# Value products of an attention unit in two steps instead of four, in a two-layer transformer kernel on one core

## The chip, the core and the metric

The kernel runs on one NeuronCore of a Trainium2 chip. The core has a matrix engine (TensorE, PE in the profile; its weight loads are the separate row kind PEld), and three engines for elementwise work: VectorE (DVE), ScalarE (ACT) and GpSimd (POOL). SyncE (SP) issues DMAs. Each engine works through its own list of instructions in order, and the engines hand over by semaphores. The metric is device time in microseconds from one launch; the time before is the median of three runs, 6809.92 us (6809.24 to 6820.73).

## The reference

Sixteen batches of 1024 tokens with 128 channels pass through a token embedding, attention layer zero (8 heads of 64, with a group norm ahead of it), a triangular MLP, attention layer one (8 heads of 16) and a top-1 mixture of 16 experts. What matters here is the attention of either layer:

```
scores = einsum('bhqe,bhke->bhqk', Q, K) * scale
attn   = softmax(scores, axis=-1)
out    = einsum('bhqk,bhke->bhqe', attn, V)
```

The kernel takes the softmax with a row maximum that is computed first, and divides by the sum at the end: the sum is an extra column of ones in V.

## The kernel before

**Units and steps.** A unit is one head and one half of its queries (512): 16 units for each batch and layer. A unit has eight steps, `kt` 0 to 7, one for each 128 keys. In each step PE makes one 128x512 tile of raw scores for a later unit's row maximum (`max_tile`, L884), then the scores of this step's keys: in layer zero two matmuls (L910 and L912), in layer one a single one (L912). DVE reduces the maximum tile (L1630), ACT takes the exponential of the scores (L1143) and writes them to `pr`. For layer zero POOL makes the low part of the exponentials (`lo_parts`, L506), four pieces a unit.

**Value products.** The products with V belong to the unit before (`at - 1`), so they run beside the scores of the present unit. `VALUE_STEPS` says in which four steps; part `j` of 0 to 3 goes to `VALUE_STEPS[j]`. For a layer-zero unit (`values0`) each part is 16 matmuls (8 pairs of L929 and L930, 128x129 in bf16) for 128 queries. For a layer-one unit (`values1`) parts 0 and 1 are four column-packed fp32 matmuls each (L945), that add up in the same bank, and part 3 is `fold1` (L955): ACT first copies the bank to `oT` (L1160), and four more matmuls then turn and sum the four quarters. Part 2 is empty there. ACT's copy stands in ACT's list at step 4 behind the exponential of that step (`OUT_STEPS = (4, 7)`).

**The banks.** Scores, maximum tiles, value outputs and the rest ("glue": projections, transposes, MLP and expert matmuls) have two PSUM banks each. So tile k of the maxima waits until tile k-2 is reduced (`max_reduced`), and the scores of step k wait until the exponential of step k-2 is done (`exp_done`).

**Segments.** The program is five segments: `first` (layer zero of batch 0), `second`, `loop` (13 turns), `penult` (each with both layers, 32 units) and `final` (layer one of the last batch). In those of two layers the units go: four of layer zero, then layer one and layer zero in turn (12 pairs), then four of layer one. Other work ("beside") is issued behind the values of a step by tables of steps: among it, in the loop, a pair of expert matmuls (L870) at steps 0 and 1 of most units, whose results DVE adds at steps 2 and 3 (L1620).

**Order inside a step on PE:** the maximum tile, the scores, the values if the step has any, the row turn (L890), the work beside.

Of the kernel before, what the change touches and what calls it, by code (L numbers as in the profile page):

```python
# [28 lines left out]
def units_of(kind):  # L29

    if kind == "first":
        return [(0, u) for u in range(16)]
    if kind == "final":
        return [(1, u) for u in range(16)]
    pairs = [unit for i in range(16 - LEAD) for unit in ((1, i), (0, LEAD + i))]
    return [(0, u) for u in range(LEAD)] + pairs + [(1, u) for u in range(16 - LEAD, 16)]
# [45 lines left out]
def due_tiles(kind, step):  # L82
    return DUE_TILES[kind].get(step, [])


def due_rows(kind, step):
    return DUE_ROWS[kind].get(step, [])
# [238 lines left out]
def build(nc, x, tok_w, gn_w, gn_b, wq, bq, wk, bk, wv, bv, wo, bo, w1, b1, w2, b2,  # L326
# [14 lines left out]
    with ExitStack() as ctx:  # L341
# [137 lines left out]
        def await_drained(eng, seg, *names):  # L479
            plan = PLANS[seg.kind][0]  # L480
            for b in range(2):
                uses = [plan[name][1] for name in names if plan[name][0] == b]
                if uses:
                    eng.wait_ge(glue_drained[b].sem, glue_drained[b].at(seg, max(uses) + 1))
# [23 lines left out]
        def steps_of(kind):  # L508
            for at, (layer, u) in enumerate(units_of(kind)):
                for kt in range(T):  # L510
                    yield 8 * at + kt, at, layer, u, kt
# [162 lines left out]
        def _(te):  # L674
# [198 lines left out]
            def max_tile(seg, when, layer, head, n):  # L873
                b = seg.layer(layer) if when == "now" else seg.following(layer)
                k = TILE_PLACES[seg.kind][when, layer, head, n]
                t, g = n // 2, n % 2
                if n == 0:
                    await_stack(te, b, layer, head)
                te.wait_ge(max_reduced.sem, max_reduced.at(seg, k - 1))
                if layer == 0:  # L880
                    qs, ks = qA[:, head % 2], kA[:, head % 2]
                else:
                    qs, ks = q_stack(1, head), k_stack(1, head)
                mm(maxb[k % 2][:, :], qs[:, t * P:(t + 1) * P], ks[:, g * HALF:(g + 1) * HALF],  # L884
                   start=True, stop=True).then_inc(max_filled.sem, 1)
# [6 lines left out]
            def tiles_and_rows(seg, step):  # L892
                for tile in due_tiles(seg.kind, step):
                    max_tile(seg, *tile)
                for it in due_rows(seg.kind, step):
                    turn_row(seg, *it)

            def turn_row(seg, when, layer, head, g):
                b = seg.layer(layer) if when == "now" else seg.following(layer)
                max_turn(seg, row_name(when, layer, head, g), b, layer, head, g)  # L900

            def scores(seg, at, layer, u, kt):
                b, k, head, g = seg.layer(layer), 8 * at + kt, u // 2, u % 2
                if kt == 0:
                    arrived = mrow_in[2 * layer + g]
                    te.wait_ge(arrived.sem, arrived.at(b, 16 * (head + 1)))
                te.wait_ge(exp_done.sem, exp_done.at(seg, k - 1))
                bank, q, kk = score[k % 2], slice(g * HALF, (g + 1) * HALF), slice(kt * P, (kt + 1) * P)
                if layer == 0:
                    mm(bank[:, :], kA[:, head % 2, kk], qA[:, head % 2, q], start=True, stop=False)  # L910
                last = max_row(0) + 1 if layer == 0 else P
                mm(bank[:, :], k_stack(layer, head)[0:last, kk], q_stack(layer, head)[0:last, q],  # L912
                   start=(layer == 1), stop=True).then_inc(score_filled.sem, 1)

            def values0(seg, at, j):
                _, u = units_of(seg.kind)[at]
                head, w = u // 2, 2 * D0 + 1
                n = o_place(seg.kind, 0, u, j // 2)
                if j == 0 and u % 4 == 0 and u > 0:
                    await_drained(te, seg, f"v0c{u // 4}.0", f"v0c{u // 4}.1")  # L920
                if j == 0:
                    te.wait_ge(lo_done.sem, lo_done.at(seg.l0, 4 * (u + 1)))
                if j % 2 == 0:
                    te.wait_ge(o_drained.sem, o_drained.at(seg, n - 1))
                dst = obank[n % 2][:, (j % 2) * 256:(j % 2) * 256 + w]
                for kt in range(T):
                    hi = pr[:, at % 2, kt, j * P:(j + 1) * P].bitcast(BF16).rearrange("p (q two) -> p q two", two=2)[:, :, 1]
                    lo = low_of(u, kt - kt % 2)[:, kt % 2, j * P:(j + 1) * P]
                    mm(dst, hi, v0[:, head // 2 % 2, kt, head % 2, 0:w], start=(kt == 0), stop=False)  # L929
                    last = mm(dst, lo, v0[:, head // 2 % 2, kt, head % 2, 0:w], start=False, stop=(kt == T - 1))  # L930
                if j % 2 == 1:
                    last.then_inc(o_filled.sem, 1)

            def values1(seg, at, j):
                _, u = units_of(seg.kind)[at]
                n = o_place(seg.kind, 1, u)
                te.wait_ge(exp_done.sem, exp_done.at(seg, 8 * at + 4 * j + 4))
                if j == 0 and u == 0:
                    await_drained(te, seg, "v1.0", "v1.1")
                if j == 0:  # L940
                    te.wait_ge(o_drained.sem, o_drained.at(seg, n - 1))
                col = (D1 + 1) * (u // 2)
                for r in range(4):
                    kt = 4 * j + r
                    last = mm(obank[n % 2][QUAD * r:QUAD * (r + 1), :], v1[:, kt, col:col + QUAD], pr[:, at % 2, kt, :],  # L945
                              start=(j == 0), stop=(j == 1))
                if j == 1:
                    last.then_inc(o_filled.sem, 1)

            def fold1(seg, at):  # L950
                _, u = units_of(seg.kind)[at]
                n = o_place(seg.kind, 1, u)
                te.wait_ge(o_hi_out.sem, o_hi_out.at(seg, n + 1))
                for t in range(4):
                    last = mm(obank[n % 2][:, QUAD * t:QUAD * (t + 1)], oT[:, t * P:(t + 1) * P], fold[:, :],  # L955
                              start=True, stop=True)
                last.then_inc(oT_turned.sem, 1)

            def values(seg, at, j):
                if units_of(seg.kind)[at][0] == 0:  # L960
                    values0(seg, at, j)
                elif j < 2:
                    values1(seg, at, j)
                elif j == 3:
                    fold1(seg, at)

            def attention(seg, *beside):
                for step, at, layer, u, kt in steps_of(seg.kind):
                    for tile in due_tiles(seg.kind, step):
                        max_tile(seg, *tile)  # L970
                    scores(seg, at, layer, u, kt)
                    if at > 0 and kt in VALUE_STEPS:
                        values(seg, at - 1, VALUE_STEPS.index(kt))
                    for it in due_rows(seg.kind, step):
                        turn_row(seg, *it)
                    for work in beside:
                        work.run(step)
                for j in range(4):
                    values(seg, at, j)
                for step in range(step + 1, LAST[seg.kind]):  # L980
                    tiles_and_rows(seg, step)
                    for work in beside:
                        work.run(step)
                if seg.nxt:
                    await_drained(te, seg, "v0c0.0", "v0c0.1")
# [735 lines left out]

LAST_STEP = 1000
LO_STEPS = (2, 4, 6)
VALUE_STEPS = (2, 3, 5, 6)
OUT_STEPS = (4, 7)
STORE_STEPS = {"loop": 191, "penult": 191, "final": 124}
SCALES = (64 ** -0.5, 1.0 / math.sqrt(16))
# [46 lines left out]
```

## Time and profile before

| what | value |
|---|---|
| median of three runs | 6809.92 us |
| profiled execution, its own time | 6804.59 us |
| its span (first to last instruction) | 6802.8 us |
| mean granted TensorE clock | 0.951 |
| PE busy | 6049.1 us, 89% |
| DVE busy | 4474.2 us, 66% |
| ACT busy | 3218.6 us, 47% |
| POOL busy | 2516.2 us, 37% |

The profiled execution lies 1.8 us above its span and 5.3 us under the median. A busy share is a mean over all stages; how close PE is to its limit within a unit is seen only in the timeline. A matmul's row shows its start and a modelled end, so that rows of PE overlap; the distance between two starts is what a matmul costs in a full queue.

### The profile page before, as it was taken

How to read it: one execution, taken by the hardware profiler on the slowest of the kernel's cores; microseconds unless marked ns; L12 is line 12 of the kernel's file. 1: busy time of each engine (PE TensorE's matmuls, PEld its weight loads, DVE VectorE, ACT ScalarE, POOL GpSimd, SP SyncE). 2: the span in 40 equal slices, each digit the busy share in tenths (PEclk: the TensorE clock that was granted, in tenths of full speed). 3: DMA queues.
4: the chain of work that ended last, by engine and by line, in shares of the span. 5: the costliest groups of instructions: out<-in, count | busy, mean ns of one | idle time of the engine just before them, and what ended most of it. 6: DMA issues, size and time to landing. Idle time of an engine off the chain costs nothing.

```text
span 6802.8 us, 126677 instructions
## 1 busy us (share of the span) xinstructions
PE 6049.1 (89%) x40167; PEld 4017.5 (59%) x40167; DVE 4474.2 (66%) x11034; ACT 3218.6 (47%) x6321; POOL 2516.2 (37%) x2135
## 2 busy tenths in 40 slices
PE   6788898998989889898998989989898998989986
PEld 4556665665656666565665656666565665656543
DVE  4456676776757667576776767767676676767664
ACT  2345545444444444554544444454544544454531
POOL 3534433433333333333433333343333433333300
PEclk7899999999999999999999999999999999999987
DMA  2121221221122121211212222121211212222110
GB/s 59 41 67 41 58 51 29 63 51 46 46 53 49 39 52 42 59 42 38 63 42 49 49 50 49 44 50 45 59 42 38 63 34 57 49 50 44 25 30 9
DMA packets 98046, 317.01 MB, mean 47 GB/s; under 512 B 27782, under 2 KB 32854, under 8 KB 87126
## 3 DMA queue, kind: packets, MB, share of 16 engines
q1 hardware_dynamic: 97366, 308.41, 19.6%
q8 instruction: 370, 6.06, 0.4%
q14 instruction: 310, 2.54, 0.1%
HBM read 57.19 MB, written 41.94 MB: 15 GB/s over the span
## 4 chain that ended last, share of the span: by engine, by line
issue 44%; POOL 25%; PE 22%; DVE 4%; ACT 2%; DMA 2%; SPq 1%; POOLq 1%; DVEq 0%; ACTq 0%
POOL pr_lo L506 21%; PE bank L884 4%; PE bank L912 3%; PE bank L945 3%; POOL on L1265 2%; PE bank L910 2%; PE bank L870 2%; PE bank L929 2%; PE bank L930 2%; DMA stacks<-parts 1%; DVE mxh L1630 1%; PE bank L719 1%; PE bank L818 1%; PE bank L708 1%; PE bank L955 1%
## 5 line engine op out<-in xcount | busy, mean ns | idle before, releaser
L1630 DVE TENSOR_REDUCE mxh<-bank 128x1 f32<-128x512 f32 x4096 | 2789.0, 688 | 1797.3 <-PE bank L884 1779.6
L1143 ACT ACTIVATE pr<-bank 128x512 f32<-128x512 f32 x4096 | 2418.4, 598 | 2723.7 <-PE bank L912 2679.9
L884 PE MATMUL bank<-stacks 128*128 128x512 f32 x4096 | 2221.3, 543 | 348.4 <-DVE mxh L1630 233.9
L506 POOL TENSOR_TENSOR pr_lo<-pr 128x1024 bf16<-128x1024 f32 x1024 | 1944.7, 1902 | 911.4 <-ACT pr L1143 909.1
L912 PE MATMUL bank<-stacks 65*128 65x512 f32 (+1 forms) x4096 | 1673.2, 409 | 27.7 <-ACT pr L1143 27.7
L884 PEld LDWEIGHTS bank<-stacks 128*128 128x128 f32 x4096 | 799.9, 195 | 1090.2 <-DVE mxh L1630 757.7
L929 PE MATMUL bank<-v,pr 128*128 128x129 bf16 x8192 | 1063.5, 222 | 94.6 <-POOL pr_lo L506 93.3
L930 PE MATMUL bank<-v,pr_lo 128*128 128x129 bf16 x8192 | 1051.1, 220 | 0.0
L929 PEld LDWEIGHTS bank<-v,pr 128*128 128x128 bf16 x8192 | 779.5, 98 | 393.1 <-issue 346.3
L1265 POOL TENSOR_TENSOR on<-on,o_r 128x128 f32<-128x128 f32 x512 | 205.4, 401 | 2045.5 <-DVE on L1660 2045.4
L912 PEld LDWEIGHTS bank<-stacks 65*128 65x128 f32 (+1 forms) x4096 | 800.2, 195 | 261.4 <-ACT pr L1143 94.4
L910 PE MATMUL bank<-stacks 128*128 128x512 f32 x2048 | 833.3, 407 | 0.2 <-ACT pr L1143 0.2
L930 PEld LDWEIGHTS bank<-v,pr_lo 128*128 128x128 bf16 x8192 | 805.2, 98 | 0.0
L870 PE MATMUL bank<-ewT,mx 128*128 128x512 f32 x1024 | 565.2, 638 | 91.7 <-DVE hm L1620 44.8
L1620 DVE SCALAR_TENSOR_TENSOR hm<-bank,wgt,hm 128x128 f32<-128x128 f32 x2048 | 571.1, 342 | 50.7 <-PE bank L870 50.7
L945 PE MATMUL bank<-pr,v 128*32 128x512 f32 x4096 | 573.6, 636 | 0.0
L910 PEld LDWEIGHTS bank<-stacks 128*128 128x128 f32 x2048 | 401.6, 196 | 133.8 <-ACT pr L1143 90.5
L955 PEld LDWEIGHTS bank<-fold,oT 128*128 128x128 f32 x2048 | 270.6, 199 | 63.0 <-ACT oT L1160 50.5
L870 PEld LDWEIGHTS bank<-ewT,mx 128*128 128x128 f32 x1024 | 183.9, 200 | 205.6 <-DVE hm L1620 68.7
L1040 ACT ACTIVATE parts<-bank,cols 128x512 fp32r<-128x512 f32 x256 | 176.4, 689 | 224.0 <-PE bank L719 213.0
L955 PE MATMUL bank<-fold,oT 128*128 128x32 f32 x2048 | 266.3, 275 | 12.6 <-ACT oT L1160 12.6
L1273 POOL TENSOR_TENSOR on<-on,o_r 128x64 f32<-128x64 f32 x256 | 75.4, 295 | 538.1 <-DVE on L1672 538.0
(170 smaller groups left out, 4925.2 us busy)
## 6 DMA issues: line engine op xcount, KB each, us to landing
stacks<-parts SPq DMA_DIRECT2D x384, 512.0 KB, 6.5
stacks<-parts_d SPq DMA_DIRECT2D x224, 128.0 KB, 3.0
parts_d<-mx SPq DMA_DIRECT2D x16, 1024.0 KB, 4.5
stacks<-parts_d SPq DMA_DIRECT2D x224, 64.0 KB, 2.8
stage<-in_pe SPq DMA_DIRECT2D x16, 512.0 KB, 7.8
stacks<-mrow SPq DMA_DIRECT2D x512, 2.0 KB
parts_d<-on SPq DMA_DIRECT2D x16, 512.0 KB, 5.2
parts_d<-stage SPq DMA_DIRECT2D x16, 512.0 KB, 6.2
```

The lines of the kernel that those rows point to most:

```text
L506: return eng.tensor_tensor(low_of(u, kt - 1).rearrange("p a b -> p (a b)"), w, hi, ALU.subtract)
L870: mm(bank[:, :], mT[:, t * P:(t + 1) * P], ewT[:, 4 * q:4 * q + 4, :].rearrange("p e f -> p (e f)"), start=True, stop=True).then_inc(fille ...
L884: mm(maxb[k % 2][:, :], qs[:, t * P:(t + 1) * P], ks[:, g * HALF:(g + 1) * HALF], start=True, stop=True).then_inc(max_filled.sem, 1)
L910: mm(bank[:, :], kA[:, head % 2, kk], qA[:, head % 2, q], start=True, stop=False)
L912: mm(bank[:, :], k_stack(layer, head)[0:last, kk], q_stack(layer, head)[0:last, q], start=(layer == 1), stop=True).then_inc(score_filled.s ...
L929: mm(dst, hi, v0[:, head // 2 % 2, kt, head % 2, 0:w], start=(kt == 0), stop=False)
L930: last = mm(dst, lo, v0[:, head // 2 % 2, kt, head % 2, 0:w], start=False, stop=(kt == T - 1))
L945: last = mm(obank[n % 2][QUAD * r:QUAD * (r + 1), :], v1[:, kt, col:col + QUAD], pr[:, at % 2, kt, :], start=(j == 0), stop=(j == 1))
L955: last = mm(obank[n % 2][:, QUAD * t:QUAD * (t + 1)], oT[:, t * P:(t + 1) * P], fold[:, :], start=True, stop=True)
L1143: act.activation(pr[:, at % 2, kt, :], score[k % 2][:, :], ACT.Exp, scale=SCALES[layer]).then_inc(exp_done.sem, 1)
L1620: ins = dve.scalar_tensor_tensor(hm[:, t, :], bank[:, e * P:(e + 1) * P], wgt[:, t, 4 * q + e:4 * q + e + 1], hm[:, t, :], ALU.mult, ALU.add)
L1630: dve.tensor_reduce(mxh[:, layer, n // 2, n % 2:n % 2 + 1], maxb[k % 2][:, :], AX_X, ALU.max)\
```

## The change

Two lines. The table of steps becomes (2, 2, 5, 5), and since a step can now have two parts, the call goes over the table instead of looking up one place.

```diff
-                    if at > 0 and kt in VALUE_STEPS:
-                        values(seg, at - 1, VALUE_STEPS.index(kt))
+                    for j, value_step in enumerate(VALUE_STEPS if at > 0 else ()):
+                        if kt == value_step:
+                            values(seg, at - 1, j)
...
-VALUE_STEPS = (2, 3, 5, 6)
+VALUE_STEPS = (2, 2, 5, 5)
```

The layer-zero unit before has 32 value matmuls in step 2 and 32 in step 5; the layer-one unit before has both accumulating groups in step 2, and its fold in step 5 in place of step 6. The lists of the other engines keep their order (ACT's copies stay at steps 4 and 7).

First place: PE's list in the second two-layer part of the program, a layer-zero unit behind a layer-one unit, from the second group of L945 to the fold. L945 is the value product, L955 the fold with `oT`; `o_hi_out` is the signal of ACT's copy to `oT`. Before:

```order
L945 MATMUL bank6<-pr,v1 32x512 [waits exp_done]
L945 MATMUL bank6<-pr,v1 32x512 x3
L884 MATMUL bank4<-stacks 128x512 [waits max_reduced]
L910 MATMUL bank2<-stacks 128x512 [waits exp_done]
L912 MATMUL bank2<-stacks 128x512
L884 MATMUL bank5<-stacks 128x512 [waits max_reduced]
L910 MATMUL bank3<-stacks 128x512 [waits exp_done]
L912 MATMUL bank3<-stacks 128x512
L884 MATMUL bank4<-stacks1 128x512 [waits max_reduced,stacks1_in0]
L910 MATMUL bank2<-stacks 128x512 [waits exp_done]
L912 MATMUL bank2<-stacks 128x512
L955 MATMUL bank6<-fold,oT 128x32 [waits o_hi_out]
```

The same stretch of PE's list in the changed kernel:

```order
L945 MATMUL bank6<-pr,v1 32x512 [waits exp_done]
L945 MATMUL bank6<-pr,v1 32x512 x3
L884 MATMUL bank5<-stacks 128x512 [waits max_reduced]
L910 MATMUL bank3<-stacks 128x512 [waits exp_done]
L912 MATMUL bank3<-stacks 128x512
L884 MATMUL bank4<-stacks 128x512 [waits max_reduced]
L910 MATMUL bank2<-stacks 128x512 [waits exp_done]
L912 MATMUL bank2<-stacks 128x512
L884 MATMUL bank5<-stacks 128x512 [waits max_reduced]
L910 MATMUL bank3<-stacks 128x512 [waits exp_done]
L912 MATMUL bank3<-stacks 128x512
L955 MATMUL bank6<-fold,oT 128x32 [waits o_hi_out]
```

The second group of L945 moved ahead of the tile and scores of step 3 (bank5 and bank3), and the fold moved ahead of those of step 6. In the first list the scores of steps 5 and 6 stand between step 4's and the fold, in the second only those of step 5.

Second place: the next unit of PE's list, a layer-one unit behind a layer-zero unit, between two blocks of value matmuls. Before, from the end of the block in step 3 to the first matmul of that in step 5:

```order
L930 MATMUL bank7<-v0,pr_lo 128x129
L884 MATMUL bank4<-stacks1 128x512 [waits max_reduced]
L912 MATMUL bank2<-stacks1 128x512 [waits exp_done]
L884 MATMUL bank5<-stacks1 128x512 [waits max_reduced]
L912 MATMUL bank3<-stacks1 128x512 [waits exp_done]
L929 MATMUL bank6<-v0,pr 128x129 [waits o_drained]
```

In the changed kernel, from the end of the block of 32 in step 2 to that in step 5:

```order
L930 MATMUL bank7<-v0,pr_lo 128x129
L884 MATMUL bank5<-stacks1 128x512 [waits max_reduced]
L912 MATMUL bank3<-stacks1 128x512 [waits exp_done]
L884 MATMUL bank4<-stacks1 128x512 [waits max_reduced]
L912 MATMUL bank2<-stacks1 128x512 [waits exp_done]
L884 MATMUL bank5<-stacks1 128x512 [waits max_reduced]
L912 MATMUL bank3<-stacks1 128x512 [waits exp_done]
L929 MATMUL bank6<-v0,pr 128x129 [waits o_drained]
```

Before, two steps without values stood between two blocks (steps 4 and 5); now it is three (steps 3, 4 and 5).

## Rows read from the trace of the kernel before

**Rows 1.** The page: busy time of each engine, and the clock in 40 slices.
```profile
PE 6049.1 (89%) x40167; PEld 4017.5 (59%) x40167; DVE 4474.2 (66%) x11034; ACT 3218.6 (47%) x6321; POOL 2516.2 (37%) x2135
...
PEclk7899999999999999999999999999999999999987
```
**Rows 2.** Groups by line: xcount | busy us, mean ns | idle before, releaser.
```profile
L1630 DVE TENSOR_REDUCE mxh<-bank 128x1 f32<-128x512 f32 x4096 | 2789.0, 688 | 1797.3 <-PE bank L884 1779.6
...
L1160 ACT ACTIVATE oT<-bank 128x512 f32<-128x512 f32 x256 | 151.8, 593 | 26.4 <-PE bank L945 26.4
...
L1152 ACT ACTIVATE o_hi<-bank 128x128 f32<-128x128 f32 x512 | 139.4, 272 | 8.0 <-PE bank L930 8.0
```
**Rows 3.** Waits of PE: total us, times, longest.
```profile
PE bank L884 <- DVE mxh L1630: 233.9, 180, 5.5
PE bank L929 <- POOL pr_lo L506: 93.3, 98, 3.6
...
PE bank L955 <- ACT oT L1160: 12.6, 16, 0.8
```
**Rows 4.** Timeline, layer-zero unit behind layer one, step 4 to the fold (start, us).
```profile
3054.81 0.40 PE L912 MATMUL bank<-stacks 65*128 65x512 f32 x1
...
3055.24 0.60 ACT L1143 ACTIVATE pr<-bank 128x512 f32<-128x512 f32 x1 [1.31 <-PE bank L912]
...
3055.50 0.40 PE L912 MATMUL bank<-stacks 65*128 65x512 f32 x1
...
3055.74 0.59 ACT L1160 ACTIVATE oT<-bank 128x512 f32<-128x512 f32 x1
...
3056.23 0.39 PE L912 MATMUL bank<-stacks 65*128 65x512 f32 x1
...
3056.38 0.97 PEld L955 LDWEIGHTS bank<-fold,oT 128*128 128x128 f32 x8 [0.19 <-ACT oT L1160]
3056.46 1.00 PE L955 MATMUL bank<-fold,oT 128*128 128x32 f32 x8
...
3057.30 0.48 PE L884 MATMUL bank<-stacks 128*128 128x512 f32 x1
```
**Rows 5.** Timeline, the same unit: the second group of L945.
```profile
3052.90 0.40 PE L912 MATMUL bank<-stacks 65*128 65x512 f32 x1
...
3053.23 0.16 PEld L945 LDWEIGHTS bank<-pr,v 128*32 128x32 f32 x8 [0.38 <-issue]
3053.23 1.07 PE L945 MATMUL bank<-pr,v 128*32 128x512 f32 x8
...
3054.23 0.50 PE L884 MATMUL bank<-stacks 128*128 128x512 f32 x1
...
3054.57 0.40 PE L910 MATMUL bank<-stacks 128*128 128x512 f32 x1
...
3054.77 1.40 DVE L1630 TENSOR_REDUCE mxh<-bank 128x1 f32<-128x512 f32 x2 [0.18 <-PE bank L884]
```
**Rows 6.** Timeline of PE, layer-one unit behind layer zero, steps 3 to 5.
```profile
3043.44 0.48 PE L884 MATMUL bank<-stacks 128*128 128x512 f32 x1
3043.75 0.40 PE L912 MATMUL bank<-stacks 128*128 128x512 f32 x1
3043.98 0.39 PE L884 MATMUL bank<-stacks 128*128 128x512 f32 x1
3044.22 0.39 PE L912 MATMUL bank<-stacks 128*128 128x512 f32 x1
3044.45 0.23 PE L929 MATMUL bank<-v,pr 128*128 128x129 bf16 x1
...
3045.34 0.48 PE L884 MATMUL bank<-stacks 128*128 128x512 f32 x1
```
**Rows 7.** Timeline of DVE in the same unit.
```profile
3042.70 0.68 DVE L1630 TENSOR_REDUCE mxh<-bank 128x1 f32<-128x512 f32 x1
3043.30 1.12 DVE L1620 SCALAR_TENSOR_TENSOR hm<-bank,wgt,hm 128x128 f32<-128x128 f32 x4
```

**Rows 8.** Waits of PE's weight loads for ACT's copy.
```profile
PEld bank L955 <- ACT oT L1160: 50.5, 130, 1.7
```

## The prediction

> **What bounds the kernel now.** I read the page first: PE is busy 89% of the span, DVE 66%, ACT 47%, POOL 37%, and the clock stands near full speed all through [rows 1]. So PE is the likely bound, but a mean over stages does not say whether it is full within a unit. The groups by line say what DVE and ACT have to do in a step: a maximum tile costs 0.688 us of DVE in each of 4096 steps, and ACT copies 256 times to `oT`, 0.593 us each [rows 2]. The waits of PE come next: in the whole program it waited 234 us for DVE's maxima, in 180 places, 93 us for POOL's low parts, and only 12.6 us for the copy to `oT`, in 16 places [rows 3]. So between these places the queue of PE is full, and the timeline shows it: in a layer-one unit the starts follow one another at 0.24 us for a matmul of 512 columns, through tile, scores and value block without a hole [rows 6]. From this I conclude that each merged block can give only what its ends cost, and that each new hole on PE lengthens the program, unless PE would have waited right behind it anyway.
>
> **The fold.** This is the largest term. Part 3 of a layer-one unit moves ahead of the tile and the scores of step 6. ACT's list stays as it was: exponential of step 4, then the copy. In the unit shown, the scores of step 4 start at 3054.81, their exponential at 3055.24, the copy runs from 3055.74 to 3056.33, and the fold starts at 3056.46, which is when the scores of step 6 (start 3056.23) let it start. Its weight load is already shown as waiting for the copy [rows 4]. So at step 6 the fold has no slack at all. At step 5 PE would come to it 0.23 us behind the scores of step 5 (start 3055.50), at 3055.73. The copy still ends at 3056.33 and the load follows 0.05 us later, at 3056.38. The hole is 3056.38 - 3055.73 = 0.65 us. Nothing fills it: the tile and scores of step 6 are queued behind the fold on PE, and DVE, ACT and POOL behind those. Taking the values out of step 3 doesn't change the hole, since the whole chain starts at the scores of step 4. What shrinks it is PE being late between the scores of steps 4 and 5, for a glue matmul in step 4 or a tile not yet reduced; this holds for some units. Bounds for the mean are 0.3 and 0.75 us (the latter where the unit above is of layer one, with one scores matmul of 0.24 us less in step 5). I take 0.5. There are 256 copies [rows 2], 16 of them in the tails of the segments behind the steps, which the table doesn't touch: 240 x 0.5 = +120 us.
>
> **The merged block of layer one.** What goes is one change to the value matmuls and back. From the scores' start to the first L945 it is 3053.23 - 3052.90 = 0.33 us, where a queue in step takes 0.23; behind the block the tile takes 3054.57 - 3054.23 = 0.34 [rows 5], again 0.1 too much. That is 0.2 us. The eight records (four matmuls, two each) take 1.00 us from the first to the next tile; with a second group right behind, the drain at the end is perhaps paid once, some 0.1 more, which no row shows. I take 0.25, with ends at 0.1 and 0.35: 240 x 0.25 = -60 us.
>
> The Trainium skill ("TensorE: Matmul & The Clock Gate", Part 3, "What overlaps and what doesn't") says that a weight load overlaps with running matmuls only where the row group differs. By that rule the second group's loads would stand open: all eight matmuls use the same 128 rows. The page's figure for a load is columns / 1.2 ns, so four loads of 32 columns would be an estimated 0.11 us a block, and the sum 26 us higher. The trace doesn't bear it out: the eight loads of one block take 0.16 us together at its start, beside matmuls that go on for 1.07 us [rows 5]. The sum goes by the row.
>
> **The merged blocks of layer zero.** Here 32 matmuls stand at step 2 and 32 at step 5. The gain: behind a block the tile takes 0.31 us to the next matmul (3043.44 to 3043.75) where it takes 0.24 in step (3043.98 to 3044.22) [rows 6], so 0.07 a block, two blocks fewer, 0.15 us a unit. The cost depends on the unit above. If it is of layer zero, a step without values is 0.7 us of PE, as long as DVE's reduction of 0.69: no hole. If it is of layer one, a step is 0.47 us (tile and one scores matmul), and three such steps in a row are more than two banks of maxima can carry. Tile k+2 waits for the reduction of tile k: a reduction starts 0.54 us behind its tile (3054.23 to 3054.77) and takes 0.7 [rows 5], so two tiles later is at the earliest 1.24 us on. In the queue it comes at 3044.45 - 3043.44 = 1.01 us, where now the block stands [rows 6]. That is a hole of 0.23 us in front of the tile of step 5. Behind the second block the same three come together (tiles of steps 6, 7 and of the next unit's 0): another 0.23. DVE's expert adds (1.12 us behind a reduction [rows 7]) are the wait's second source: today the block of step 3 covers the one in step 3, afterwards it falls in the bare steps. It is queued ahead of the reduction of tile 4, which is wanted only behind the block at step 5, so I put it at nothing; without that cover it costs up to 0.5 us a unit. The holes are filled where a glue matmul stands in these steps, as it does in perhaps a third of the units.
> - 195 units of layer zero have a layer-one unit above (12 pairs and the first of the last four, in 15 segments): (0.67 x 0.46 - 0.15) = 0.16 us each, +31 us. Ends: -0.15 (no hole) and +0.5.
> - 60 have a layer-zero unit above (15 in the first segment, 3 in each of 15 others): 60 x -0.15 = -9 us.
>
> **Edits at nothing.** POOL's low parts: the block at step 2 waits for the same piece as today (98 waits, 93 us [rows 3]); the merged half needs no later one. ACT's waits for filled banks (8 us for `o_hi` [rows 2]) go to zero, off the path. `pr` comes free a step earlier; no exponential waits for it. No DMA or SP instruction moves. The drained bank for the second half is that of the unit before, read out at its step 7, long before step 5.
>
> **Sum.** 120 - 60 + 31 - 9 = +82 us. The profiled execution took 6804.6 us, so it would be 6887; the median of the runs shown is 5.3 us higher: 6892. I forecast **6892 us**, 1.2% more.
>
> **Rivals.**
> - *The holes are absorbed, and the merged blocks win.* If PE would wait for DVE behind the fold anyway, the 0.65 us only moves the wait. For it: 234 us of such waits exist. Against: they are 180 places in 4096 steps [rows 3], so most of the 240 folds have none behind them. Then only the gains stand, -60 - 255 x 0.15 = -98 us: 6712. It decides if the starts behind the fold (tile of step 6, 7) today already have holes of half a us in most units; those in the unit shown have none [rows 4].
> - *Gains and holes cancel.* The fold's hole at its lower end (0.3), the block of layer one at its upper (0.35), no hole in the bare steps: 72 - 84 - 38 = -50; with the hole at 0.5, 120 - 84 - 38 = -2 us. The time is then 6808. For it: the drain of the L945 block is not shown by a row.
> - *The bursts starve DVE and ACT more than two tiles' worth.* During 32 matmuls (1.8 us) DVE has at most one tile and one set of adds, then all its work comes at once; the hole at the fold is full (0.65) and each layer-zero unit under layer one pays 0.5: 156 - 48 + 98 - 9 = +197 us: 7007. For it: DVE is busy for 66% of the span already [rows 1], and all of that is to fit beside fewer, longer blocks. Against: a backlog on DVE holds PE only in the bare steps, and DVE is idle 1797 us ahead of its reductions for want of a tile [rows 2].
> - *The change doesn't reorder PE.* Excluded by the lists of instructions shown with the change.
>
> **How the numbers follow.** Forecast (holes at the fold exceed what merging saves): 0.70, own range 6840 to 6960. Starved bursts: 0.14. Cancel: 0.08. Absorbed: 0.08. The range 6825 to 6985 leaves out the absorbed case, the upper part of the starved one and half of the cancelling one. A measurement of this kernel can tell about 0.2% (14 us) from no change. Faster by more: 0.09. Within: 0.06. Slower by more: 0.85.
>
> **What would show it.** Waits of PE (weight load and matmul) for ACT's `oT` should go from 51 us in 130 places for the loads and 13 us for the matmuls [rows 3, 8] to over 100 us in all, with a count near 240. In the unit's timeline the fold starts 1.6 us behind the scores of step 4, as before, but only one scores matmul stands between, and the tile of step 6 follows it. L945 should come as a block of 16 records of 1.8 to 1.9 us. Waits of L884 for DVE rise in layer-one units at steps 5 and 0 by 0.2 us each. Should the wait for `oT` stay small, or the distance between the scores of steps 4 and 5 grow to 1.3 us by other waits, the first term is wrong. Should L945 blocks be twice 1.0 us plus the same ends, the second is.

## The result, and the profile after

The changed kernel takes 6928.8 us (median of 4 runs, 6925.88 to 6943.78), the kernel before 6810.0 us: a ratio of 1.0174, with an interval of 1.0158 to 1.0190. The forecast was 6892 us, the range 6825 to 6985. The profiled execution has a span of 6924.1 us, 121.3 more than before. The page of the changed kernel, to be read beside [rows 1], with the groups that answer to [rows 2] (lines of DVE and ACT are one higher than before):

```profile
PE 6096.8 (88%) x40167; PEld 4098.5 (59%) x40167; DVE 4435.4 (64%) x11034; ACT 3213.9 (46%) x6321; POOL 2502.3 (36%) x2135
...
PEclk8899999999999999998999999999999999999987
...
L1631 DVE TENSOR_REDUCE mxh<-bank 128x1 f32<-128x512 f32 x4096 | 2773.7, 688 | 2013.3 <-PE bank L884 2003.6
...
L955 PEld LDWEIGHTS bank<-fold,oT 128*128 128x128 f32 x2048 | 251.4, 191 | 200.0 <-ACT oT L1161 196.7
L955 PE MATMUL bank<-fold,oT 128*128 128x32 f32 x2048 | 273.4, 277 | 94.8 <-ACT oT L1161 94.5
```

The counts of instructions are those of before, so no engine has more to do; DVE idles 216 us longer in front of its reductions (2013.3 against 1797.3), for want of a tile. That PE is nevertheless busy 47.7 us longer with the same 40167 records points to its clock. The profile records which of two levels was granted (1.2 or 2.4 GHz): PE stood at the lower for 671 us in total before and for 741 us now (mean granted clock 0.951 and 0.946). At the lower level the distance from L910 to L912 is 0.43 us in place of 0.23 (medians, kernel before), so at most half of such time is lost: up to 35 of the 121.3 us. In the turns of the loop it falls in units 0 to 8 and 22 to 31; in the units 9 to 21 of every turn the full clock is granted, in all kernels of this document.

The waits, against [rows 3, 8] (total us, times, longest):

```profile
PEld bank L884 <- DVE mxh L1631: 529.1, 982, 5.1
...
PEld bank L955 <- ACT oT L1161: 196.7, 222, 1.7
PE bank L884 <- DVE mxh L1631: 188.0, 162, 5.0
...
PE bank L955 <- ACT oT L1161: 94.5, 193, 0.8
PE bank L929 <- POOL pr_lo L506: 88.1, 100, 3.6
```

The fold's loads wait 222 times in place of 130. PE's long waits for DVE's maxima did not rise (188.0 us in place of 233.9); the many short ones that were added lie inside the modelled length of the matmuls and are seen only as distances between starts. Three places of the timeline show them. First the fold, in the changed kernel, against [rows 4] (start, us):

```profile
3093.67 0.39 PE L912 MATMUL bank<-stacks 65*128 65x512 f32 x1
...
3094.40 0.40 PE L912 MATMUL bank<-stacks 65*128 65x512 f32 x1
...
3094.60 0.59 ACT L1161 ACTIVATE oT<-bank 128x512 f32<-128x512 f32 x1
...
3095.24 1.08 PE L955 MATMUL bank<-fold,oT 128*128 128x32 f32 x8 [0.43 <-ACT oT L1161]
...
3096.15 0.48 PE L884 MATMUL bank<-stacks 128*128 128x512 f32 x1
```

PE is free for the fold 0.23 us behind the scores of step 5, at 3094.63, and starts it at 3095.24, 1.57 us behind the scores of step 4: a hole of 0.61 us, with the tile of step 6 behind it. Second, the merged group of layer one, against [rows 5]:

```profile
3090.24 0.39 PE L912 MATMUL bank<-stacks 65*128 65x512 f32 x1
...
3090.55 1.92 PE L945 MATMUL bank<-pr,v 128*32 128x512 f32 x16
...
3091.44 0.13 PEld L945 LDWEIGHTS bank<-pr,v 128*32 128x32 f32 x4 [0.30 <-issue]
...
3092.41 0.19 PEld L884 LDWEIGHTS bank<-stacks 128*128 128x128 f32 x1 [0.84 <-issue]
3092.41 0.50 PE L884 MATMUL bank<-stacks 128*128 128x512 f32 x1
```

Sixteen records take 1.86 us to the next tile, where two blocks of eight took 1.00 each. Third, the bare steps of a layer-one unit, against [rows 6, 7]:

```profile
3081.52 0.48 PE L884 MATMUL bank<-stacks 128*128 128x512 f32 x1
...
3082.03 0.69 DVE L1631 TENSOR_REDUCE mxh<-bank 128x1 f32<-128x512 f32 x1 [0.63 <-PE bank L884]
3082.07 0.40 PE L884 MATMUL bank<-stacks 128*128 128x512 f32 x1
...
3082.30 0.40 PE L912 MATMUL bank<-stacks 128*128 128x512 f32 x1
...
3082.78 0.19 PEld L884 LDWEIGHTS bank<-stacks 128*128 128x128 f32 x1 [0.52 <-DVE mxh L1631]
3082.78 0.50 PE L884 MATMUL bank<-stacks 128*128 128x512 f32 x1
...
3083.12 0.40 PE L912 MATMUL bank<-stacks 128*128 128x512 f32 x1
```

The tile of step 5 (3082.78) comes 1.26 us behind that of step 3 (3081.52), not 1.01. The scores follow 0.34 us on, not 0.24, since the load behind a wait has nothing to hide under: the hole is 0.35 us. The same stands at the end of the unit.

### The profile page after: what moved, and what is told of

It reads as the page before. It is cut to its first block, busy times and chain, and to the rows that moved or that the text cites. A ratio compares the mean times of both kernels' runs of the same rounds, so it can differ in the third digit from the quotient of the medians.

```text
span 6924.1 us, 126677 instructions
## 1 busy us (share of the span) xinstructions
PE 6096.8 (88%) x40167; PEld 4098.5 (59%) x40167; DVE 4435.4 (64%) x11034; ACT 3213.9 (46%) x6321; POOL 2502.3 (36%) x2135
## 4 chain that ended last, share of the span: by engine, by line
issue 45%; POOL 24%; PE 21%; DVE 5%; ACT 3%; DMA 1%; POOLq 1%; SPq 0%; DVEq 0%; ACTq 0%
POOL pr_lo L506 20%; PE bank L884 4%; PE bank L945 3%; PE bank L912 3%; POOL on L1266 2%; PE bank L870 2%; PE bank L910 2%; PE bank L929 2%; PE bank L930 2%; DVE mxh L1631 1%; DMA stacks<-parts 1%; PE bank L955 1%; PE bank L719 1%; PE bank L818 1%; DVE hm L1621 1%
## 5 line engine op out<-in xcount | busy, mean ns | idle before, releaser
L1631 DVE TENSOR_REDUCE mxh<-bank 128x1 f32<-128x512 f32 x4096 | 2773.7, 688 | 2013.3 <-PE bank L884 2003.6
L884 PE MATMUL bank<-stacks 128*128 128x512 f32 x4096 | 2214.1, 541 | 301.7 <-DVE mxh L1631 188.0
L912 PE MATMUL bank<-stacks 65*128 65x512 f32 (+1 forms) x4096 | 1673.8, 409 | 27.8 <-ACT pr L1144 27.8
L929 PE MATMUL bank<-v,pr 128*128 128x129 bf16 x8192 | 1010.2, 222 | 89.4 <-POOL pr_lo L506 88.1
L930 PE MATMUL bank<-v,pr_lo 128*128 128x129 bf16 x8192 | 1004.6, 221 | 0.0
L912 PEld LDWEIGHTS bank<-stacks 65*128 65x128 f32 (+1 forms) x4096 | 800.3, 195 | 273.9 <-ACT pr L1144 103.9
L929 PEld LDWEIGHTS bank<-v,pr 128*128 128x128 bf16 x8192 | 794.0, 98 | 244.9 <-issue 207.0
L910 PE MATMUL bank<-stacks 128*128 128x512 f32 x2048 | 837.5, 409 | 0.7 <-ACT pr L1144 0.7
L945 PE MATMUL bank<-pr,v 128*32 128x512 f32 x4096 | 546.7, 655 | 0.0
L910 PEld LDWEIGHTS bank<-stacks 128*128 128x128 f32 x2048 | 403.7, 197 | 147.7 <-ACT pr L1144 106.7
L955 PEld LDWEIGHTS bank<-fold,oT 128*128 128x128 f32 x2048 | 251.4, 191 | 200.0 <-ACT oT L1161 196.7
L955 PE MATMUL bank<-fold,oT 128*128 128x32 f32 x2048 | 273.4, 277 | 94.8 <-ACT oT L1161 94.5
L945 PEld LDWEIGHTS bank<-pr,v 128*32 128x32 f32 x4096 | 112.8, 116 | 278.4 <-issue 244.7
```

The source lines that it names most:

```text
L1631: dve.tensor_reduce(mxh[:, layer, n // 2, n % 2:n % 2 + 1], maxb[k % 2][:, :], AX_X, ALU.max)\
```

## Experiments

Units without other work in these steps repeat to 0.04 us from turn to turn of the loop, so each kernel can be read in two of them: the layer-one unit behind a layer-zero unit (18th place, from 0) and the layer-zero unit next to it (19th). The table gives the distance from the unit's first scores to the next unit's, as the sum of the medians over the 13 turns of the distances between starts of L912. The last column has the time at the lower clock in the profiled execution. The ratios are taken against executions of the kernel before from the same session (medians 6805.6 to 6810.0), so differences of medians across rows are good to some 4 us.

| kernel | median us | ratio, interval | 18th | 19th | low clock, us |
|---|---|---|---|---|---|
| before | 6810 | | 9.68 | 10.53 | 671 |
| changed | 6928.8 | 1.0174, 1.0158 to 1.0190 | 10.35 | 10.89 | 741 |
| layer zero merged alone | 6874.8 | 1.0098, 1.0066 to 1.0130 | 10.28 | 10.53 | 719 |
| layer one merged alone, fold at 5 | 6858.3 | 1.0074, 1.0053 to 1.0096 | 9.77 | 10.91 | 693 |
| layer one merged alone, fold at 6 | 6881.1 | 1.0109, 1.0089 to 1.0129 | 9.70 | 10.92 | 792 |
| the same, some adds a step later | 6814.1 | 1.0015, 1.0003 to 1.0027 | 9.69 | 10.15 | 696 |
| changed, copy at 3 | 6801.0 | 0.9986, 0.9976 to 0.9996 | 10.33 | 10.18 | 700 |
| copy at 3, layer zero merged only under layer zero | 6708.6 | 0.9854, 0.9839 to 0.9868 | 9.77 | 10.19 | 658 |
| the same with (2, 2, 4, 6) under layer one | 6757.0 | 0.9936, 0.9921 to 0.9952 | 10.25 | 10.16 | 688 |
| before, half reductions | 6712.9 | 0.9863, 0.9847 to 0.9879 | 9.68 | 10.52 | 651 |
| changed, half reductions | 6777.6 | 0.9956, 0.9940 to 0.9972 | 10.21 | 10.87 | 635 |
| before, layer zero merged only under layer zero | 6787.3 | 0.9975, 0.9963 to 0.9987 | 9.68 | 10.52 | 717 |
| before, only the last part moved there | 6786.7 | 0.9970, 0.9950 to 0.9990 | 9.68 | 10.52 | 697 |

**The two halves of the change.** For most of the experiments `VALUE_STEPS` is looked up by the layer of the unit whose values they are, and by the layer of the unit above:

```diff
+                    of, under = (units_of(seg.kind)[at - 1][0] if at > 0 else 0), layer
-                    for j, value_step in enumerate(VALUE_STEPS if at > 0 else ()):
+                    for j, value_step in enumerate(VALUE_STEPS[of][under] if at > 0 else ()):
...
+VALUE_STEPS = (((2, 2, 5, 5), (2, 2, 5, 5)), ((2, 3, 9, 6), (2, 3, 9, 6)))   # layer zero merged alone
+VALUE_STEPS = (((2, 3, 5, 6), (2, 3, 5, 6)), ((2, 2, 9, 5), (2, 2, 9, 5)))   # layer one merged alone
```

> Layer zero alone is merged (steps 2, 2, 5, 5); layer one stands as before (2, 3, fold 6). Theory: the merged blocks of layer zero save 0.14 us a unit and open two holes of 0.35 us where the unit above is of layer one, clean in two thirds of 195 units, +95 us; under a layer-zero unit they gain, some -38 us in all. Sum +57 us: 6867 (6850 to 6885). Rival: the whole loss is the fold's, the merged blocks of layer zero cost nothing: 6771 to 6810.

> Layer one alone is merged (both groups at step 2, fold at 5); layer zero stands as before. Theory: the hole in front of the fold, 0.67 us in clean units and less in others, minus 0.35 us a unit that the merged group saves: 119 - 57 = +62 us, 6872 (6850 to 6890). Rival (the holes of both parts cover one another, so that each alone costs nearly as much as both): 6900 or more.

Measured: 6874.8 and 6858.3, both within what the first theory gave. The spans are 62.7 and 52.2 us above that of before, 114.9 together, of 121.3 for both. The parts add up, and neither covers the other (up to 24 and 11 us of them are the lower clock's): layer zero lengthens the 18th unit alone, layer one the 19th (and the 18th by 0.09).

**Layer one merged, the fold left at step 6.**

```diff
-VALUE_STEPS = (((2, 3, 5, 6), (2, 3, 5, 6)), ((2, 2, 9, 5), (2, 2, 9, 5)))
+VALUE_STEPS = (((2, 3, 5, 6), (2, 3, 5, 6)), ((2, 2, 9, 6), (2, 2, 9, 6)))
```

> Layer one's groups both at step 2, but the fold stays at step 6; layer zero as before. Theory: only the saving of the merged group is left, 240 x 0.35 = -84 us: 6726 (6715 to 6750), faster than before. Rival: taking 1.2 us out of step 3 starves PE between steps 3 and 6 (bare steps, DVE's reductions), and the saving is eaten: 6790 to 6815.

Measured: 6881.1, and the theory falls. The saving in step 3 is there, but the 19th unit is as long as with the hole. The timeline of this kernel shows what holds it:

```profile
3080.24 0.40 PE L884 MATMUL bank<-stacks 128*128 128x512 f32 x1
...
3080.58 1.12 DVE L1622 SCALAR_TENSOR_TENSOR hm<-bank,wgt,hm 128x128 f32<-128x128 f32 x4
...
3081.43 0.40 PE L912 MATMUL bank<-stacks 65*128 65x512 f32 x1
3081.61 1.28 DVE L1632 TENSOR_REDUCE mxh<-bank 128x1 f32<-128x512 f32 x2
...
3082.35 0.50 PE L884 MATMUL bank<-stacks 128*128 128x512 f32 x1 [0.52 <-DVE mxh L1632]
```

Tile 4 stands ready at 3080.24, but DVE has the expert adds of step 3 ahead of its reduction, which starts at 3081.61. The tile of step 6, due 0.23 us behind the scores of step 5 (3081.43), starts at 3082.35, 0.69 us late. Before, the block in step 3 stood in between; with it the same step had no hole (the scores of step 6 came 0.73 us behind those of step 5, here 1.49). A fold at step 5 covers it too, since it fills PE for 0.8 us in front of that tile.

This hole is not the whole of the loss. Of the 76.4 us of span above the kernel before, up to 60 are the lower clock's (792 us at it in place of 671), 36 of them in the last units of the 13 turns.

**The adds behind the reduction, in four units of a segment.**

```diff
-                            yield AT[f"e{n}.1"] + 2
+                            yield AT[f"e{n}.1"] + (3 if seg.kind != "final" and n in (1, 3, 11, 13) else 2)
```

> The kernel with layer one merged and the fold at step 6 (6881), and DVE's second half of the expert adds moved from step 3 to step 4 in four of the 16 pairs (the units 9, 11, 19 and 21 of a segment). Theory: there the tile of step 6 waits 0.77 us because the reduction of tile 4 stands behind the adds of step 3; with the adds behind that reduction the hole closes in these four units, in 14 segments: 56 x 0.77 = -43 us, 6838 (6825 to 6850), and the other units keep it. Rival: the hole comes from ACT or from the scores' banks: no change, 6881.

Measured: 6814.1. In the four units, the 19th among them, the distance falls by 0.74 to 0.77 us, and in the timeline of this kernel both reductions run first:

```profile
3051.87 1.39 DVE L1632 TENSOR_REDUCE mxh<-bank 128x1 f32<-128x512 f32 x2 [1.01 <-PE bank L884]
...
3053.17 1.11 DVE L1622 SCALAR_TENSOR_TENSOR hm<-bank,wgt,hm 128x128 f32<-128x128 f32 x4
...
3053.56 0.40 PE L884 MATMUL bank<-stacks 128*128 128x512 f32 x1
...
3054.17 0.97 PEld L955 LDWEIGHTS bank<-fold,oT 128*128 128x128 f32 x8 [0.19 <-ACT oT L1162]
```

The mechanism is confirmed for these units: they give 39.6 us in the 13 turns, as expected. But the whole fell by 67 us, where 43 were expected. The rest lies mainly in the last unit of a turn, and the granted clock goes with it. One turn as an example, from the unit's first scores to the next unit's (window, length; PE's busy time and records; granted clock; DMA share, GB/s), the first row before, the second with the fold at 6, the third with the adds later:

```profile
2790.42:2816.52 26.10, 18.29 (x88) 0.87 0.03 7
2813.56:2843.78 30.22, 21.18 (x88) 0.72 0.03 7
2787.91:2812.81 24.90, 16.28 (x88) 0.91 0.03 8
```

Over all 13 turns these units take 333.8, 367.4 and 327.3 us, and the lower clock costs up to 41.8, 77.4 and 31.7 us of it: the fold at 6 lengthens them by 33.6 us and the later adds shorten them by 40.1, no more than the clock can account for. The same 88 records stand in all three. What made the clock fall more often there was not tried; PE is idle for about a third of these units in all three kernels.

**ACT's copy a step earlier.** The changed kernel with one move in ACT's list:

```diff
+                    if at > 0 and units_of(seg.kind)[at - 1][0] == 1 and kt == 3:
+                        outputs1(seg, at - 1)
-                    if at > 0 and kt in OUT_STEPS:
+                    if at > 0 and units_of(seg.kind)[at - 1][0] == 0 and kt in OUT_STEPS:
                         outputs(seg, at - 1, OUT_STEPS.index(kt))
```

> The changed kernel with one move on ACT: the copy of a layer-one unit's bank stands behind the exponential of step 3, not of step 4. The fold stays at step 5. Theory: the hole in front of the fold is the distance from the scores of step 4 to the end of the copy; with the copy a step earlier it closes, about -145 us against the changed kernel: 6783 (6765 to 6805). Rival: DVE, late by the bare steps, holds PE there anyway, and the time stays at 6900 or above.

Measured: 6801.0, some 128 us below the changed kernel, and the span 124.6 below. In the timeline the copy runs beside step 5 and the fold follows its scores without a hole (3051.93 + 0.23):

```profile
3051.43 0.59 ACT L1161 ACTIVATE oT<-bank 128x512 f32<-128x512 f32 x1
...
3051.93 0.39 PE L912 MATMUL bank<-stacks 65*128 65x512 f32 x1
...
3052.16 1.00 PE L955 MATMUL bank<-fold,oT 128*128 128x32 f32 x8
...
3052.99 0.48 PE L884 MATMUL bank<-stacks 128*128 128x512 f32 x1
```

This is the price of the fold's hole, with everything else in place; up to 21 us of it is the lower clock's (741 us at it, then 700). DVE doesn't take over.

**What paces the bare steps.** Two kernels take the maximum over half of a tile, so that a reduction takes 0.42 us and not 0.69; they leave out half of the keys in the row maximum:

```diff
-                dve.tensor_reduce(mxh[:, layer, n // 2, n % 2:n % 2 + 1], maxb[k % 2][:, :], AX_X, ALU.max)\
+                dve.tensor_reduce(mxh[:, layer, n // 2, n % 2:n % 2 + 1], maxb[k % 2][:, 0:256], AX_X, ALU.max)\
```

> The kernel before, with each maximum taken over half of the tile's columns (256 of 512), which leaves out half of the keys in the row maximum: a control, to see what a shorter reduction gives by itself. PE is full in the clean units, so only the waits of PE for maxima (234 us in all, some of them for other reasons) can shrink: 6740 to 6800.

> The changed kernel with the same half reductions. Theory: the holes of the bare steps (0.35 us twice in 195 units, clean in two thirds, some 95 us) are DVE's pace and close; the fold's hole is ACT's chain and stays. So against the control it is +25 us (0 to +50) where the full reductions gave +119. Rival: the bare steps are paced by ACT's exponentials and the two banks of scores: +119 against the control again.

Measured: 6712.9 and 6777.6, a difference of 65 us, between the theory (25) and the rival (119); the control, too, fell further than expected (97 us). The totals mislead here, since the clock differs too. The spans lie 74 us apart, and up to 82 with the lower clock taken out of both; full reductions gave 121, and 86 without it. So most of the drop from 119 to 65 can be the clock's, and half reductions took off little else. The clean units have the full clock, and in them each was half right, as the timeline of the changed kernel with half reductions shows at the tile and scores of step 5:

```profile
3017.59 0.42 DVE L1631 TENSOR_REDUCE mxh<-bank 128x1 f32<-128x256 f32 x1 [0.90 <-PE bank L884]
...
3018.07 0.19 PEld L884 LDWEIGHTS bank<-stacks 128*128 128x128 f32 x1 [0.25 <-DVE mxh L1631]
3018.08 0.48 PE L884 MATMUL bank<-stacks 128*128 128x512 f32 x1
3018.48 0.19 PEld L912 LDWEIGHTS bank<-stacks 128*128 128x128 f32 x1 [0.22 <-ACT pr L1144]
3018.48 0.49 PE L912 MATMUL bank<-stacks 128*128 128x512 f32 x1
```

The tile no longer waits to speak of, but the scores now wait for the exponential of step 3, and come 1.09 us behind its scores (3017.39). The hole of step 5 shrinks from 0.35 to 0.16 us, that at the end of the unit only from 0.37 to 0.33, and the step with the second double block grows by 0.09. In all the 18th unit is 0.53 us longer than in the control, where full reductions made it 0.67. So the bare steps stand under two limits close together, DVE's pair of tiles (1.26 us) and ACT's pair of scores (1.09 us).

**Layer zero merged only under layer zero.** With the holes placed, the next kernel keeps the savings and leaves out what opens the second kind of hole: copy at 3, layer one merged with the fold at 5, and

```diff
+VALUE_STEPS = (((2, 2, 5, 5), (2, 3, 5, 6)), ((2, 2, 9, 5), (2, 2, 9, 5)))
```

> Layer one merged (both groups at step 2), ACT's copy at step 3, fold at 5; layer zero merged (2, 2, 5, 5) only where the unit above is of layer zero too, elsewhere as before (2, 3, 5, 6). Theory: this keeps every saving that the runs so far showed and opens no hole: 6801 less the 95 us that the merged layer-zero blocks cost under layer-one units, 6706 (6690 to 6730). Rival: the savings of layer one were the cover of the bare steps, and with the old steps back DVE holds the tile of step 5 or 6 anyway: 6780 or more.

Measured: 6708.6, 1.5% faster than before, within 3 us of the expectation. Its span is 93.6 us below that with all layer-zero blocks merged: the price of the merged blocks under layer one, with up to 21 us of lower clock in it.

> The kernel of 6709 us (layer one merged, copy at step 3, layer zero merged under layer zero) with (2, 2, 4, 6) in place of (2, 3, 5, 6) for a layer-zero unit under a layer-one unit: one double block, and at most two bare steps between blocks. Theory: one change of kind less (0.07 us in 195 units, -14 us), but the tile of step 6 waits for the reduction of tile 4 behind the adds of step 3, as with the fold at step 6: up to +0.4 us in some 130 units. Sum +30 us: 6740 (6705 to 6770). Rival (only the number of bare steps counts): 6695.

Measured with (2, 2, 4, 6) in place of (2, 3, 5, 6): 6757.0, 48 us more. The double block saves (steps 2 and 3 together take 2.82 us with both blocks in step 2, 2.90 with one in each), but in the 18th unit the one step without values between two blocks, from the scores of 5 to those of 6, takes 1.02 us, where the one between the scores of 4 and 5 took 0.46. The wait is again that for a reduction behind the adds:

```profile
2608.61 1.12 DVE L1624 SCALAR_TENSOR_TENSOR hm<-bank,wgt,hm 128x128 f32<-128x128 f32 x4
...
2609.65 0.68 DVE L1634 TENSOR_REDUCE mxh<-bank 128x1 f32<-128x512 f32 x1
...
2610.39 0.50 PE L884 MATMUL bank<-stacks 128*128 128x512 f32 x1 [0.28 <-DVE mxh L1634]
```

Few bare steps in a row are not enough; what DVE has queued in them counts.

**The units under layer zero.** Only 60 units change, from the kernel before:

```diff
+VALUE_STEPS = (((2, 2, 5, 5), (2, 3, 5, 6)), ((2, 3, 9, 6), (2, 3, 9, 6)))   # merged
+VALUE_STEPS = (((2, 3, 5, 5), (2, 3, 5, 6)), ((2, 3, 9, 6), (2, 3, 9, 6)))   # last part alone
```

> The kernel before with one thing changed: a layer-zero unit's values are merged (2, 2, 5, 5) where the unit above is of layer zero too (60 of 255 units). Theory: -38 us, 6770 (6760 to 6785); 0.07 us for each of two blocks that go in 60 units is 9 us of it, the rest comes from PE's waits for the stack DMA in two units of each turn, in front of the tile of step 6, which now have one value block less behind them. Rival: the 28 us that this class lost in the loop are made elsewhere (later waits) and come back here: 6800 or more.

> The same, but under a layer-zero unit only the last quarter moves, from step 6 to step 5 (2, 3, 5, 5); the first two blocks stay apart. Theory (the gain is a block moved in front of a wait that doesn't depend on PE): nearly all of the gain stays, -33 us, 6775 (6765 to 6790). Rival (merging at step 2 makes the gain): -9 us or less, 6800.

Measured: 6787.3 (0.9975, 0.9963 to 0.9987) and 6786.7 (0.9970, 0.9950 to 0.9990). The last part alone gives all of it, so it isn't merging that helps, but the move in front of a wait. The two timelines of the third unit of a turn show which; before, and then the changed kernel:

```profile
2849.17 1.11 PE L839 MATMUL bank<-wo_sb,mx 128*128 128x128 f32 x8
2852.19 0.49 PE L884 MATMUL bank<-stacks 128*128 128x512 f32 x1 [1.91 <-DMA stacks<-parts]
```

```profile
2884.77 1.11 PE L839 MATMUL bank<-wo_sb,mx 128*128 128x128 f32 x8
2886.89 0.49 PE L884 MATMUL bank<-stacks 128*128 128x512 f32 x1 [1.01 <-DMA stacks<-parts]
```

The tile of step 6 waits for a DMA whose time PE doesn't set. A block of 0.9 us that is done before the wait costs nothing. PE's waits for this DMA fall by 11 us in all, before and with the merged blocks:

```profile
PE bank L884 <- DMA stacks<-parts: 64.1, 23, 8.8
```

```profile
PE bank L884 <- DMA stacks<-parts: 52.9, 23, 8.9
```

But the gain was half of the 38 us expected. In the profiled execution of the merged kernel the summed distances of the 60 units fall by 29 us, and 13 come back in the others. The clock is enough for that: outside the 60 units, where the lists are those of before, up to 31 us more are lost to it. The 11 executions of this kernel say the same: the one with a mean clock of 0.951 took 6769.4 us, the two with 0.945 and 0.946 took 6803.1 and 6793.6. Why a change in 60 units lowers the clock in later ones stays open.

## Why the prediction was right

The sign, the main mechanism and the range were right; the sizes of the terms were off, the granted clock was missing, and the errors partly cancelled. The spans split the change: the changed kernel stands 121.3 us above before, the copy at 3 takes off 124.6, unmerging under layer one another 93.6, the 60 units under layer zero gave 18 (by medians) in their own runs, and the rest is put down to layer one, with the errors of all the others in it. The last column is the most that the lower clock can be of each: half of the difference in time at it.

| term | predicted | measured | clock in it, at most |
|---|---|---|---|
| the fold's hole | +120 | +125 | +21 |
| layer one's merged group (the rest) | -60 | -79 | -30 |
| layer zero under layer one | +31 | +94 | +21 |
| layer zero under layer zero | -9 | -18 | +23 |
| sum | +82 | +121 | +35 |

- *The clock at nothing.* The prediction read it as near full speed all through and gave it no term. It can be up to 35 us of the change. With all of it taken out the sum would be 86 us, near the forecast of 82, but that is luck: the terms would be +104, -49, +72 and -41.
- *The fold.* Right in place, cause and size (0.5 us a copy was taken; 125 us over 240 copies are 0.52, without the clock 0.43). The hole of 0.65 us was read off the chain from the scores of step 4 to the end of the copy; it measured 0.61 from PE being free to the fold, and 0.68 in the distance between the scores of steps 5 and 6 (2.30 us against 1.62 with the copy at 3), since the fold's load lies bare as well.
- *The merged group.* The saving was put at 0.25 us with an end at 0.35; in the 19th unit it is 0.37 (3.81 us for the two steps before, 2.75 + 0.69 after). The drain, which no row of before showed, is real: 1.86 us for sixteen records against 2 x 1.00. The load rule of the Trainium skill ("TensorE: Matmul & The Clock Gate", Part 3, "What overlaps and what doesn't") did not bind: the later loads, four at a time, took 0.13 us beside running matmuls, and the second group cost 0.86 us, less than the first.
- *Layer zero under layer one: the term that was furthest off.* The text said two holes of 0.23 us in two thirds of the units, 0.16 us net, which is 0.31 us in a unit with both. Where the holes lie was right, and so was the wait for the tile (1.26 us, 1.24 predicted). The size left out the load that a wait lays bare, 0.1 us each time: a hole is 0.35 (0.81 us for the step, 0.46 before). The 18th unit grew by 0.60 us where layer zero alone was merged, twice the 0.31. The 94 us in all are three times the 31, and still 72 without the clock.
- *The adds at nothing.* They were priced at nothing because only a tile behind the block at step 5 needs them out of the way. That held in the 18th and 19th unit of the changed kernel. The fold at step 6 and (2, 2, 4, 6) showed the cost without that cover: 0.77 and 0.56 us a unit.
- *Layer zero under layer zero.* Counted as two switches only; the wait for the stack DMA, which stood in the waits of PE (64 us in 23 places), had not been looked up by its place. The 60 units gained 29 us in the profiled execution, not 9.
- *The rival of absorbed holes* was decided by what stands behind the fold. With the copy at 3 the hole closed in full, so nothing had absorbed it. But the fold at step 6 is a case of it turned round: there DVE's wait took the place of ACT's.

## What to carry to other kernels

Where an engine is full, as PE is in these units, merging blocks of its work won only the ends of the blocks, and lost where the steps in between became shorter than what the other engines need for as many buffers as there are. Before a consumer is moved ahead, follow the chain of its input from the last instruction that this chain shares with the mover, and move the copy that feeds it by as much. The same merge can be right beneath one neighbour and wrong beneath another: here a table by neighbour and a copy one step earlier turned +1.7% into -1.5%. And before a difference of some tens of us between two kernels is put down to a wait, compare the time that each spent at the lower clock: two sums here that did not come out, for the later adds and for the 60 units, are off by no more than it allows.

## What had not been expected of the hardware

- A 512-column matmul whose weight load had to wait costs 0.34 us to the next, in place of 0.24: the wait lays bare part of the load (start to start, 3082.78 to 3083.12).
- Four column-packed fp32 matmuls behind four others on the same columns cost 0.86 us more (1.86 - 1.00), less than the first four with their ends (1.2); here one group of eight in place of two of four saved 0.37 us a unit.
- The maxima over half of a tile save 1.4% of the whole (6712.9 us) though the 18th and 19th unit stay as long as before (9.68 and 10.52): what they save lies in other units.
- Moving a few value blocks changed the clock that PE was granted elsewhere. With the fold at step 6 the last units of the turns hold the same 88 records as before, and run up to 36 us longer for the clock alone; the time at the lower clock ranges from 635 to 792 us over the kernels here.
